# Attention sums moved by DMA inside the loop, inverted and scaled a batch later, and projected in the same block

## What is computed

```python
qkv = (x @ Wqkv + bqkv).reshape(B, L, 3, n_heads, head_dim)      # 4, 1024, 3, 16, 8
q, k, v = (qkv[:, :, 0], qkv[:, :, 1], qkv[:, :, 2])
scores = jnp.einsum('bqhd,bkhd->bhqk', q, k) / math.sqrt(head_dim)
scores = scores + slopes[None, :, None, None] * bias[None, None]
probs = jax.nn.softmax(scores, axis=-1)
out = jnp.einsum('bhqk,bkhd->bqhd', probs, v).reshape(B, L, D)
return out @ Wout + bout
```

## Time and profile before

| what | us |
|---|---|
| median of 3 runs | 3477.67 (3476.5 to 3478.36) |
| profiled execution | 3491.22 |
| its span, first to last instruction | 3489.5 |
| TensorE busy | 2953.6 (85%) |
| ScalarE busy | 2352.7 (67%) |
| VectorE busy | 2203.5 (63%) |
| GpSimd busy | 411.4 (12%) |

### The profile page before, as it was taken

The page is one execution under the profiler, slowest core; times in us unless marked ns, Lnnn a source line. Parts: engine busy times, 40 slices in busy tenths (PEclk is TensorE's granted clock), DMA queues, the critical chain, the costliest instruction groups (busy, mean ns, idle before and its releaser), DMA issues. The chain is left out here.

```text
span 3489.5 us, 54163 instructions
## 1 busy us (share of the span) xinstructions
PE 2953.6 (85%) x18300; PEld 1343.2 (38%) x18300; DVE 2203.5 (63%) x3764; ACT 2352.7 (67%) x3403; POOL 411.4 (12%) x245
## 2 busy tenths in 40 slices
PE   4888888899998498898899999787868656999997
PEld 2221223566665211111356666522236441111116
DVE  5777777677776777777767777677789862000004
ACT  5789987555454699999655544464624447999992
POOL 2000000000000400000000000065634320000002
PEclk8899999999999799999999999899979867999996
DMA  5433441000000634333100000000000004222210
GB/s 121 57 53 50 59 59 20 25 0 1 0 0 5 171 48 55 53 52 49 29 6 0 1 0 0 26 1 0 0 0 0 0 14 99 41 41 37 42 29 27
DMA packets 68365, 111.08 MB, mean 32 GB/s; under 512 B 10656, under 2 KB 22944, under 8 KB 67312
## 3 DMA queue, kind: packets, MB, share of 16 engines
q1 hardware_dynamic: 68176, 108.58, 18.4%
HBM read 80.85 MB, written 27.69 MB: 31 GB/s over the span
## 5 line engine op out<-in xcount | busy, mean ns | idle before, releaser
L1660 ACT ACTIVATE m_mix_hidden<-m_mix_up_ps 128x512 f32<-128x512 f32 x512 | 305.5, 597 | 294.5 <-PE m_mix_up_ps L1604 294.5
L935 ACT ACTIVATE b_direct_probs<-b_direct_s_ps 128x1024 f32<-128x1024 f32 x512 | 473.6, 1094 | 14.3 <-PE b_direct_o_ps L883 11.7
L1612 PE MATMUL m_mix_down_ps<-m_w,m_mix_hidden 128*128 128x128 f32 x4096 | 474.8, 276 | 0.0
L935 ACT ACTIVATE c_att_probs<-c_att_s_ps 128x1024 f32<-128x1024 f32 x512 | 470.3, 1219 | 5.9 <-PE c_att_o_ps L883 4.1
L1612 PEld LDWEIGHTS m_mix_down_ps<-m_w,m_mix_hidden 128*128 128x128 f32 x4096 | 467.2, 192 | 15.3 <-issue 15.3
L1604 PE MATMUL m_mix_up_ps<-m_mix_ZT,m_w 128*128 128x512 f32 x1024 | 470.5, 617 | 0.3 <-ACT m_mix_hidden L1660 0.3
L935 ACT ACTIVATE a_direct_probs<-a_direct_s_ps 128x1024 f32<-128x1024 f32 (+10 forms) x512 | 431.5, 939 | 56.1 <-DVE a_direct_s_ps L964 42.2
L964 DVE SCALAR_TENSOR_TENSOR a_direct_s_ps<-distance,slopes,a_direct_s_ps 128x512 f32<-128x512 f32 (+3 forms) x512 | 355.4, 732 | 121.8 <-PE a_direct_s_ps L863 119.1
L961 DVE TENSOR_TENSOR b_direct_s_ps<-b_direct_s_ps,distance 128x512 f32<-128x512 f32 x512 | 336.0, 695 | 141.1 <-PE b_direct_s_ps L863 140.8
L950 DVE COPY c_out_t<-c_att_o_ps 128x512 f32 x32 | 22.1, 692 | 465.4 <-PE c_att_o_ps L883 465.2
L883 PE MATMUL b_direct_o_ps<-b_direct_probs,v_cols 128*32 128x512 f32 x2048 | 274.4, 608 | 14.1 <-DVE b_out_t L950 13.1
(11 more groups left out here) (330 smaller groups left out, 3511.7 us busy)
## 6 DMA issues: line engine op xcount, KB each, us to landing
qk_parts<-b_qkv_parts SPq DMA_DIRECT2D x48, 256.0 KB, 3.1
qk_parts<-a_qkv_parts SPq DMA_DIRECT2D x24, 256.0 KB, 3.6
a_k_rows<-qk_parts SPq DMA_DIRECT2D x32, 192.0 KB
a_q_rows<-qk_parts SPq DMA_DIRECT2D x32, 192.0 KB
b_k_rows<-qk_parts SPq DMA_DIRECT2D x32, 192.0 KB
b_q_rows<-qk_parts SPq DMA_DIRECT2D x32, 192.0 KB
qk_parts<-c_split_parts SPq DMA_DIRECT2D x24, 256.0 KB, 3.0
c_k_rows<-qk_parts SPq DMA_DIRECT2D x32, 192.0 KB
```

The lines of the kernel that those rows point to most:

```text
L935: act.activation(probs[:, J % 2, j, lo:hi], s_ps[:, slot(hg, n), lo:hi], ACT.Exp).then_inc(exped, 1)
L1612: last = pe.matmul(down_ps[:, t % 2, e, :], hidden[:, e * HALVES + h, t * P:(t + 1) * P], w["w2"][:, e * HALVES + h, :], start=(h == 0), s ...
L1660: act.activation(hidden[:, f, :], up_ps[:, f % UP_BANKS, :], ACT.Silu).then_inc(silu_done, 1)
```

## The change

- `take_sums` now copies into `taken`, two slots of 1024 columns, one for even and one for odd groups. It waits until the slot's former content has been moved.
- On SP, `move` takes each group from its slot by five DMAs: four bring the 8 rows of each head to their 8 partitions of `joined` (128 partitions by all 4096 tokens), one stores the four rows of sums in DRAM. These stand in SP's queue ahead of the operand loads.
- One batch later, `gather` reads the 16 rows of sums back as 128 partitions by 128, `invert` on VectorE takes the reciprocals, `keep` stores them, `spread_out` reads them with each row repeated for the 8 partitions of its head, and `scale` on VectorE multiplies the batch in `joined` by them. On SP these three DMAs stand in the steps `hg` 2, 3 and 4 of the next batch, on VectorE the two instructions stand behind unit 24 of groups 1 and 3 (in c behind the copies of those groups).
- GpSimd adds the output bias to a batch of X in the loop.
- Behind the loop, in the same block, TensorE multiplies `joined` by the output weight (in c it transposes `joined`) into the free PSUM slots, and VectorE adds the result to X, in 8 steps. Six of them belong to batches 0 to 2; they stand ahead of the last batch's inversion.
- `normalise` is gone, and `project_out` and the new `turn_heads` are used by the general branch only.

```diff
-def attend_transposed(nc, tag, V, operands, out_t, ident, table=None, slopes=None, span=None):
+def attend_transposed(nc, tag, V, operands, joined, ident, table=None, slopes=None, span=None, X=None, w_out=None,
+                      b_out=None, kept=None):
...
+    def result(n):
+
+        b, half = divmod(n, 2)
+        return o_ps[:, half, :] if b == BATCH - 1 else s_ps[:, b, half * BANK:(half + 1) * BANK]
...
+        taken = k.sb(f"{tag}_taken", [P, 2, SEQ])
+        dense = k.sb(f"{tag}_dense", [P, SEQ * HEADS // P])
+        inverse = k.sb(f"{tag}_inverse", [P, SEQ])
...
         @block.sync
         def _(sp):
+            def move(b, hg, past=0):
+
+                sp.wait_ge(o_out, b * (2 * HG) + (2 * hg + 6 - past * 2 * HG))
+                at = bass.ds(b * SEQ - past * SEQ, SEQ)
+                for j in range(GH):
+                    to = slice((hg * GH + j) * HD, (hg * GH + j + 1) * HD)
+                    sp.dma_start(joined[to, at], taken[VW * j:VW * j + HD, hg % 2, :]).then_inc(moved[hg % 2], 16)
+                sp.dma_start(sums_dram[bass.ds(b * HEADS + (hg * GH - past * HEADS), GH), :],
+                             taken[HD:P:VW, hg % 2, :]).then_inc(sums_kept[hg % 2], 16)
...
+            def gather(b):
+                for half in range(2):
+                    sp.wait_ge(sums_kept[half], b * 32)
+                src = of_batch(sums_dram, b).rearrange("h (c t) -> (h c) t", c=P // HEADS)
+                sp.dma_start(dense[:, :], src).then_inc(gathered, 16)
+
+            def keep(b):
+                sp.wait_ge(inverted, b * 1)
+                dst = of_batch(inverse_dram, b).rearrange("h (c t) -> (h c) t", c=P // HEADS)
+                sp.dma_start(dst, dense[:, :]).then_inc(inverse_kept, 16)
+
+            def spread_out(b):
+                sp.wait_ge(inverse_kept, b * 16)
+                sp.dma_start(inverse[:, :], of_batch(inverse_dram, b).unsqueeze(1).to_broadcast([HEADS, HD, SEQ])
+                             ).then_inc(spread, 16)
...
-            with sp.Fori(0, BATCH - 1) as b:
+            def batch(b, first, final):
                 for hg in range(1, HG + 1):
-                    ahead(b, hg)
-            for hg in range(1, HG):
-                ahead(BATCH - 1, hg)
+                    if hg >= 2:
+                        move(b, hg - 2)
+                    elif not first:
+                        move(b, HG - 1, 1)
+                    if not first and hg >= 2:
+                        (gather, keep, spread_out)[hg - 2](b)
+                    if not (final and hg == HG):
+                        ahead(b, hg)
+
+            batch(0, True, False)
+            with sp.Fori(1, BATCH - 1) as b:
+                batch(b, False, False)
+            batch(BATCH - 1, False, True)
+            move(BATCH - 1, HG - 1)
+            gather(BATCH)
+            keep(BATCH)
+            spread_out(BATCH)
...
+                if b_out is not None:
+                    x = X[:, bass.ds(b * TPB, TPB), :]
+                    pool.tensor_tensor(x, x, over_mid(b_out, TPB), ALU.add).then_inc(biased_x, 1)
...
+            def finish(n):
+                pe.wait_ge(scaled, n // 2 + 1)
+                if n // 2 == BATCH - 1:
+                    pe.wait_ge(o_out, BATCH * (2 * HG) + 4)
+                else:
+                    pe.wait_ge(exped, BATCH * NB + SLOTS)
+                for t in range(4):
+                    at = (4 * n + t) * P
+                    to = result(n)[:, t * P:(t + 1) * P]
+                    if w_out is None:
+                        last = pe.transpose(to, joined[:, at:at + P], ident)
+                    else:
+                        last = pe.matmul(to, joined[:, at:at + P], w_out, start=True, stop=True)
+                last.then_inc(projected, 1)
...
             def take_sums(b, hg, c):
                 if c == 0:
                     dve.wait_ge(left_summed, b * HG + (hg + 1))
+                    if hg >= 2 or not isinstance(b, int) or b:
+                        dve.wait_ge(moved[hg % 2], b * (2 * MOVES) + hg // 2 * MOVES)
+                        dve.wait_ge(sums_kept[hg % 2], b * 32 + hg // 2 * 16)
                 else:
                     dve.wait_ge(summed, b * (HG * JT) + (hg * JT + JT + 2))
-                dst = out_t[:, bass.ds(b + hg * BATCH, 1), c * BANK:(c + 1) * BANK].rearrange("p o q -> p (o q)")
+                dst = taken[:, hg % 2, c * BANK:(c + 1) * BANK]
                 dve.tensor_copy(dst, o_ps[:, c, :]).then_inc(o_out, 1)
...
+            def invert(b):
+                dve.wait_ge(gathered, b * 16 + 16)
+                dve.reciprocal(dense[:, :], dense[:, :]).then_inc(inverted, 1)
+
+            def scale(b):
+                for half in range(2):
+                    dve.wait_ge(moved[half], b * (2 * MOVES) + 2 * MOVES)
+                dve.wait_ge(spread, b * 16 + 16)
+                out = joined[:, bass.ds(b * SEQ, SEQ)]
+                dve.tensor_tensor(out, out, inverse[:, :], ALU.mult).then_inc(scaled, 1)
+
+            def add(n):
+                dve.wait_ge(projected, n + 1)
+                x = X[:, 4 * n:4 * n + 4, :]
+                dve.tensor_tensor(x, x, result(n).rearrange("p (t d) -> p t d", d=D), ALU.add)
...
+                        if not first and n == SCALE_AT and hg == 1:
+                            invert(b - 1)
+                        if not first and n == SCALE_AT and hg == HG - 1:
+                            scale(b - 1)
...
+            early = 2 * (BATCH - 1)
+            for n in range(early):
+                add(n)
+            invert(BATCH - 1)
+            scale(BATCH - 1)
+            for n in range(early, early + 2):
+                add(n)
...
-            def direct():
-                with ExitStack() as inner:
-                    out_t = Kit(nc, inner).sb(f"{tag}_out_t", [P, (HEADS // GH) * BATCH, SEQ])
-                    attend_transposed(nc, f"{tag}_direct", V, operands, out_t, ident, table=const.distance,
-                                      slopes=const.slopes, span=alibi_span)
-                    normalise(nc, f"{tag}_norm", out_t, out, ident)
...
+                attend_transposed(nc, f"{tag}_direct", V, operands, joined, ident, table=const.distance,
+                                  slopes=const.slopes, span=alibi_span, X=X, w_out=w["out"], b_out=w["b_out"], kept=const.kept_sums)
```

More of the change, by code:

```diff
@@ L794, in attend_transposed @@
     TAKE_AT = (4, 7)
+    SCALE_AT = 24
     SIDE = SEQ // 2
@@ L972, in batch @@
                         take_sums(b, hg, 1)
+                        if hg == 1 and not first:
+                            invert(b - 1)
+                        if hg == HG - 1 and not first:
+                            scale(b - 1)
                         continue
@@ L1051, in _ @@
         def _(pe):
-            def turn(s):
+            for s in range(STEPS):
                 if s >= 2:
@@ L1055, in turn @@
                 for t in range(4):
[L1056 removed]
+                    last = pe.transpose(t_ps[:, s % 2, t, :], out[:, 4 * s + t, :], ident)
                 last.then_inc(turned, 1)
[L1058 to L1067 removed]
         @block.scalar
```

144 lines of the change are left out of this document (66 added, 78 removed).

## The result

The changed kernel takes 3535.8 us (median of 4 runs, 3523.3 to 3538.4) against 3477.1 for the kernel before in the same comparison (3474.3 to 3478.4): a ratio of 1.016, 95% interval 1.014 to 1.019. It is slower, by 58.7 us between the medians; the forecast was 3466.0 in 3457 to 3477. The profiled executions span 3521.5 us after and 3489.5 before.

The account below looks back on a forecast made before the run. ScalarE's exponentials bound the attention loops, with 77.8 us of serial tails behind them. Tails gain 17.4 us, loops lose 5.8: 11.6 off the profiled 3491.2 gives 3479.6, or 3466.1 as the runs' median; range 3457 to 3477.

Parts of the forecast that it names:

- So they may be 5.2 us later: Operand loads in a's loop: they stopped moving by 211.0, their first matmul ran at 216.23, so 5.2 us of slack.
- That just fits: A batch's last step in a and b: five issues plus the spread delay loads 4.8 us, leaving 0.4 us, four times.
- I count nothing here: SP's queue in the loops: DMAs added ahead of the operand loads were given no cost in the sum.
- Five issues: SP's queue ahead of each group's loads: five issues with dynamic addresses take 2.5 us.
- the spread is slow, loads late: Third rival: spread at about 100 GB/s, tails 9.9 us longer, four late loads cost 11.6 us; 3488 us, chance 0.13.
- The sign that the prediction named for itself: In the new profile: wrong if a batch's first matmul waits on operand loads, or the end chain takes over 24 us.
- the new tails: Serial chain from last copy of sums to last add: 20.6 us in a and b, 19.1 in c, 17.4 gained together.
- the last 16 passes: TensorE's last two projection steps in the tails of a and b: 3.5 us, between 2.04 at full clock and 3.9.
- the moves' issue: Start of the tail: SP issues four moves, then the sums' store, the fifth DMA going out 1.9 us after the last copy.
- the gather: In the tail: reading 64 KB of sums from DRAM takes 2.9 us, from the time of a bias load.
- VectorE's cost in the loops: Inversion and scaling for batches 1 to 3 stop ScalarE: 2.6 us in b, 3.2 in a, sum 5.8; bounds 0 and 13.0.
- a drift of either sign: The two lora stages: shifting c's end may move either by a few us, with either sign.

Follow-up runs that it names:

- the run with moves alone: The kernel before, plus four moves and the sums' store to scratch ahead of each group's loads, no gather, store, spread or VectorE work: 3549.5 us, ratio 1.020.
- the loads first and VectorE late: The changed kernel with operand loads ahead of its other DMAs in SyncE's queue and the inversion and scaling moved later: 3463.7 us, ratio 0.995.
- four tiny stores: The kernel before with four DMAs of 4 partitions x 64 bytes to unread DRAM ahead of each group's loads: 3483.8 us, ratio 1.002.

## Why the prediction was wrong

1. **The step that failed** is "So they may be 5.2 us later", and with it "That just fits" and "I count nothing here". It read the slack at one boundary and took it for all. By the semaphore's record the slack there was 3.5 us, and at the other thirteen of a it was 0.0 to 1.9, against a delay of 3.4 to 5.1 us. In the changed kernel the boundary in the place of the earlier trace rows is the only one of the 14 without a wait: its loads leave at 198.47, are ready 17.3 us later, and the matmul comes 2.0 us after that. The term put at nothing measured 45.5 + 19.2 = 64.7 us in the two loops, some 60 without VectorE's 4.9. The kernel before already had waits for loads at two boundaries of a, where every 0.1 us of delay counted. The prediction did not look at them:

```profile
PEld a_direct_s_ps L863 <- DMA a_k_rows<-bias_rows: 1.6, 1, 1.6
...
PE a_direct_s_ps L863 <- DMA a_k_rows<-bias_rows: 1.5, 2, 1.3
```

2. **At the boundary it read, 5.2 us was too much as well.** It took the loads as ready when no data moved in a window, 17.3 us after the first issue. A window counts a piece of a transfer where the piece begins: the last one of those loads began at 210.97 and ended at 212.05, and the semaphore was last raised at 212.68. That leaves 3.5 us until 216.23. The same is seen around a wait of the changed kernel (last columns: granted clock, DMA share, GB/s):

```profile
278.00:279.00 1.00, 0.55 (x5) 0.10 (x2) 0.58 (x2) 1.00 (x2) 0.00 (x0) 1.00 0.38 82
279.00:280.00 1.00, 0.00 (x0) 0.00 (x0) 0.34 (x1) 1.00 (x2) 0.00 (x0) 1.00 0.07 8
280.00:281.00 1.00, 0.00 (x0) 0.00 (x0) 0.00 (x0) 0.40 (x1) 0.00 (x0) 0.89 0.00 0
281.00:282.00 1.00, 0.55 (x3) 0.12 (x4) 0.00 (x0) 0.00 (x0) 0.00 (x0) 0.50 0.00 0
```

 Here the last piece ended at 280.44, the semaphore was last raised at 281.34, and the matmul ran at 281.45. The Trainium skill (DMA: Bandwidth & Descriptors, Anatomy of one DMA — SWDGE (gpsimd) path) says of the other descriptor path that the semaphore cannot be updated until the last byte is confirmed in the target memory, and gives that most of a fixed 2 us. The traces agree in kind, with less: 0.6 and 0.9 us from the last piece's end to the last raising. The prediction had fixed costs in the new chain and left them out of the loads.

3. **The term was mis-sized too.** Five issues were put at 2.5 us, for which no row stands; the first load left 3.5 us late in the group above and up to 5.0 (433.70 to 438.65) where one of the round trip followed. The two middle batches were slower than the first and last even without it: 4.2 to 4.4 us for most groups of the run with moves alone, for 3.4 to 3.6. A move took 0.65 us to issue and the sums' store 0.54 to 0.62, where the loads stood 0.42 apart.

4. **The rival** "the spread is slow, loads late" had the right wait, with a chance of 0.13, and the wrong reach: it counted four late groups in both stages, behind a spread, and 11.6 us. TensorE was late at thirteen of a's 14 boundaries, and the two loops grew by 65 us. Its own mechanism was a small part: b's two longest waits, behind a spread. The spread itself was not slow, so its price of a longer tail did not come. The sign that the prediction named for itself, the wait turning to the operand loads, did come.

5. **Right**: the new tails, 19.6, 19.5 and 18.0 us for 20.6, 20.6 and 19.1. The spread landed after 4.7 us for 4.6, the last 16 passes took 3.78 for 3.5, the inversion 0.95; of the terms the moves' issue was 1.0 us longer and the gather 1.1 shorter, the others within 0.4 us. The terms of that chain, as written, add up to 20.4 and 18.9; 0.2 stands without a term. The last matmuls ran at a granted 0.50, as said. VectorE's cost in the loops: 4.9 for 5.8, in part by luck, since ScalarE's last exponential of b began at 1702.84 and not at 1703.02, 0.04 us behind VectorE and not 0.22 (the row's eight exponentials overlap, so an eighth of it is not the length of one). With the loads first and VectorE late the kernel reaches 3463.7, 2.3 us below the forecast of 3466.0. That agreement is of the sum without the failed step, and it is loose: no cost of VectorE shows in that kernel's loops, and its last stage, which the change leaves alone, was 4.8 us shorter than before.

What stays open: how b's 19.2 us divide between the delay in the queue and the spread's data, since no run has the round trip by itself or a delay of 4 to 5 us with nothing else; and how much of a's growth is the lower clock.

## What to carry to other kernels

A queue that prefetches just in time has its slack at the tightest boundary. Read the waits list for a wait on it that is already there, take the slack at every boundary and not at one, and count readiness to the instruction that was released, not to the last byte moved. Put what nobody waits for behind the prefetches; then look what it in turn holds up, since the small DMA behind them lands late, and move its reader back. An added DMA costs its issue time in the queue, even with 64 bytes a row.

## What the runs showed of the hardware

- A move's issue time did not depend on its bytes: 0.65 us (median of 64) with 32 KB and with 0.5 KB, and the loads behind four of them and the sums' store were as late (3.55 us at 135.25, 3.54 at 130.07). Other forms took other times: most loads 0.3 to 0.4 us, four tiny stores 1.27.
- A gather of 64 KB released its reader 1.8 us after its issue at the end of a stage and 12.6 behind 14 loads.
- TensorE's granted clock fell within a wait of 2.91 us in the loop: 1.00 before 280, 0.89, then 0.50 in the window of 281 (2.4 to 1.2 GHz). The eight passes after it took 1.93 us for 1.07; at 287.66 eight took 1.07 again. It also fell about 1 us after the end of the shorter wait at 153.44 (1.91 us), with matmuls running: 0.75 in the window of 154, 0.50 in that of 155.
- A stage that the change doesn't touch took another time. The last stage's 256 passes, before and after:

```profile
3429.00:3489.00 60.00, 47.91 (x256) 43.84 (x256) 22.02 (x55) 19.65 (x63) 9.41 (x4) 0.61 0.13 35
```

```profile
3471.00:3521.00 50.00, 38.05 (x256) 35.04 (x256) 22.41 (x52) 18.84 (x60) 9.40 (x4) 0.77 0.15 43
```

 The mean granted clock is 0.61 before and 0.77 after, and from its first pass to the end the stage takes 50.2 us for 59.5. That is 9.3 us of the 33.0, which the prediction had left as a drift of either sign. Over all profiled executions it takes 50.2 to 54.7 us in the seven kernels with the new end of c, and 59.5 or 59.6 in three of the five with the old one, but 51.8 and 54.7 in the other two. So it is a drift that may lean to the new end, and no gain to be counted on.
